# Queries directly behind the outputs, all eight tiles of values together behind the scores

## What is computed

```
xn = group_norm(x, gamma, beta)            # 32 groups, eps 0.001
q = xn @ wq + bq;  k = xn @ wk + bk;  v = xn @ wv + bv
scores = einsum('bnc,bmc->bnm', q, k) * C ** (-0.5)
attn = softmax(scores, axis=-1)
out = einsum('bnm,bmc->bnc', attn, v)
out = out @ wp + bp + x
```

## Time and profile before

| | |
|---|---|
| median of three runs | 2090.53 us (2090.38 to 2091.23) |
| the profiled execution, its own time | 2090.45 us |
| its span, first to last instruction | 2088.7 us |
| PE busy | 2082.3 us, 9214 matmuls |
| DVE busy | 1734.4 us |
| ACT busy | 746.2 us |
| POOL busy | 535.0 us |

### The profile page before, as it was taken

The page is one execution under the profiler, slowest core; times in us unless marked ns, Lnnn a source line. Parts: engine busy times, 40 slices in busy tenths (PEclk is TensorE's granted clock), DMA queues, the critical chain, the costliest instruction groups (busy, mean ns, idle before and its releaser), DMA issues.

```text
span 2088.7 us, 28028 instructions
## 1 busy us (share of the span) xinstructions
PE 2082.3 (100%) x9214; PEld 1724.0 (83%) x9214; DVE 1734.4 (83%) x2838; ACT 746.2 (36%) x1225; POOL 535.0 (26%) x236
## 2 busy tenths in 40 slices
PE   9999999999999999999999999999999999999999
PEld 7888888888888888888888888888888888888887
DVE  7997888878889788897878888788887888878864
ACT  5332423335233252333423333243333523325231
POOL 1323123322132212322223231322322213221230
PEclk9999999999999999999999999999999999999999
DMA  7212030120301203021120211203012030120201
GB/s 177 61 51 71 6 91 25 50 70 10 109 2 57 63 15 105 0 80 40 34 87 0 80 40 50 70 0 92 28 50 70 10 98 13 50 70 14 67 1 61
DMA packets 110331, 108.13 MB, mean 52 GB/s; under 512 B 8540, under 2 KB 74080, under 8 KB 110304
## 3 DMA queue, kind: packets, MB, share of 16 engines
q1 hardware_dynamic: 108544, 104.63, 16.8%
q10 hardware_dynamic: 1760, 3.15, 0.6%
HBM read 74.19 MB, written 33.55 MB: 52 GB/s over the span
## 4 chain that ended last, share of the span: by engine, by line
PE 99%; DVE 1%; DMA 0%; issue 0%; SPq 0%; ACT 0%; DVEq 0%
PE psum L1375 11%; PE psum L1376 11%; PE psum L1377 11%; PE psum L1356 11%; PE psum L1358 11%; PE psum L1357 11%; PE psum L1141 6%; PE psum L1143 6%; PE psum L1142 6%; PE psum L1245 5%; PE psum L1244 5%; PE psum L1242 5%; DMA w_k<-in_L_conv_wk_dram 0%; PE psum L1196 0%; PE psum L1198 0%; PE psum L1197 0%
## 5 line engine op out<-in xcount | busy, mean ns | idle before, releaser
L449 POOL TENSOR_TENSOR x_res<-x_res,out_bias 128x512 f32<-128x512 f32 x124 | 216.1, 1766 | 895.9 <-PE psum L1245 451.0
L1375 PE MATMUL psum<-v_hi,pt_hi 128*128 128x512 f32 x1024 | 398.4, 389 | 0.0
L1376 PE MATMUL psum<-v_lo,pt_hi 128*128 128x512 f32 x1024 | 398.3, 389 | 0.0
L1377 PE MATMUL psum<-v_hi,pt_lo 128*128 128x512 f32 x1024 | 398.3, 389 | 0.0
L585 ACT ACTIVATE score<-psum 128x512 f32<-128x512 f32 x256 | 152.8, 597 | 325.1 <-PE psum L1358 325.0
L1375 PEld LDWEIGHTS psum<-v_hi,pt_hi 128*128 128x128 f32 x1024 | 192.2, 188 | 39.9
L1377 PEld LDWEIGHTS psum<-v_hi,pt_lo 128*128 128x128 f32 x1024 | 192.2, 188 | 39.9
L1376 PEld LDWEIGHTS psum<-v_lo,pt_hi 128*128 128x128 f32 x1024 | 192.2, 188 | 39.9
L1356 PE MATMUL psum<-pt_hi,xn_hi 128*128 128x512 f32 x512 | 199.5, 390 | 0.4 <-DVE v_lo L834 0.4
L1358 PE MATMUL psum<-pt_hi,xn_lo 128*128 128x512 f32 x512 | 199.2, 389 | 0.0
L1357 PE MATMUL psum<-pt_hi,xn_hi 128*128 128x512 f32 x512 | 199.2, 389 | 0.0
(11 more groups left out here) (184 smaller groups left out, 3942.6 us busy)
## 6 DMA issues: line engine op xcount, KB each, us to landing
x_res<-in_x_dram SPq DMA_DIRECT2D x128, 256.0 KB, 2.9
out_dram<-x_res SPq DMA_DIRECT2D x128, 256.0 KB, 2.1
x_blk<-in_x_dram SPq DMA_DIRECT2D x240, 128.0 KB, 2.8
score<-in_x_dram SPq DMA_DIRECT2D x16, 128.0 KB, 6.7
w_q<-in_L_conv_wq_dram ACTq DMA_DIRECT2D x6, 256.0 KB, 10.8
w_v<-in_L_conv_wv_dram SPq DMA_DIRECT2D x1, 1024.0 KB, 5.8
w_p<-in_L_conv_wp_dram SPq DMA_DIRECT2D x1, 1024.0 KB, 9.3
w_k<-in_L_conv_wk_dram ACTq DMA_DIRECT2D x4, 256.0 KB, 9.0
```

What stands on the lines that cost most here:

```text
L449: last = nc.gpsimd.tensor_tensor(at, at, out_bias[:, first:end], ALU.add)
L1375: nc.tensor.matmul(dst, hi[:, m, queries], v_hi[:, m, :], start=m == 0, stop=False)
L1376: nc.tensor.matmul(dst, hi[:, m, queries], v_lo[:, m, :], start=False, stop=False)
L1377: end = nc.tensor.matmul(dst, lo[:, m, queries], v_hi[:, m, :], start=False, stop=m == NT - 1)
```

## The change

Only the order is changed, and what follows from it for banks and semaphores; no instruction is added or dropped but waits.

- In every image the values of tiles 0 and 1 are moved from in front of the queries to the front of the other six, behind the scores, on PE, ACT and DVE.
- In image 0 the two halves of the queries so stand directly behind one another. Both now use `work[0]` to `work[3]`, and chunk j of the second half waits for `first_query_lo(0, j)`.
- The banks of the later queries are renamed so that each still precedes the score tile that uses the same bank. Waits on `v_lo` in the queries fall away but for the first; a wait for the whole `xn_lo` takes the place of the one that tile 0 of the values had.
- On DVE in image 0, `m_lo` parts 2 and 3 are made behind all first queries and `xn_lo`; and the four `first_query_lo(1, j)` stand ahead of the four `row_part(0, j)` and are no longer interleaved with them.

```
-        USES = ([("v", 0, m) for m in range(2)] + [("s", h, m) for h in range(NH) for m in range(NT)]
-                + [("v", 0, m) for m in range(2, NT)])
+        USES = [("s", h, m) for h in range(NH) for m in range(NT)] + [("v", 0, m) for m in range(NT)]
...
         def first_bank(h, j):
-            return work[(2 * h + j) % 4]
+            return work[j]
...
             def first_queries():
                 first_query_lo(0, 0)
-                setup_lo_parts(SET_M, m_hi, m_lo, 3, KC)
                 first_query_lo(0, 1)
                 second_lo_parts()
                 first_query_lo(0, 2)
                 first_query_lo(0, 3)
-                v_lo_part(0, 0)
-                v_lo_part(0, 1)
+
+                setup_lo_parts(SET_M, m_hi, m_lo, 2, KC)
                 block_sums_of_a()
...
                 for j in range(KC):
                     first_query_lo(1, j)
+                for j in range(KC):
                     row_part(0, j)
...
                     else:
 
                         pe.wait_ge(s_free, n * SPLIT)
+                        pe.wait_ge(s_xl, (n + 1) * KC)
                     block_product(BANK_1, A11, p, xn_hi, xn_lo, 0, 0)
...
                 for j in range(KC):
-                    if j < 2:
-                        pe.wait_ge(s_tl, j + 3)
-                    else:
-
-                        pe.wait_ge(s_free, j - 1)
+
+                    pe.wait_ge(s_tl, j + 1)
...
                 if starts(b):
                     first_half_queries()
-                v_tile(b, 0)
-                v_tile(b, 1)
-                if starts(b):
                     second_half_queries()
                 else:
                     queries(b)
                 for m in range(NT):
                     score_tile(b, 0, m)
                 for m in range(NT):
                     score_tile(b, 1, m)
-                for m in range(2, NT):
+                for m in range(NT):
                     v_tile(b, m)
```

More of the change, by code:

```diff
@@ L246, in group_norm_attention @@
         assert NU % 4 == 0 and NU == SPLIT + SCORES
-        BANK_1, BANK_6, BANK_7, BANK_5 = work[2], work[3], work[0], work[1]
+        BANK_1, BANK_6, BANK_7, BANK_5 = work
         def final_half(n, h):
@@ L661, in image @@
                     bias_products()
-                v_hi_part(b, 0)
-                v_hi_part(b, 1)
-                if starts(b):
                     for j in range(KC):
@@ L1020, in _ @@
             sum_products(0, KC)
-            setup_lo_parts(SET_M, m_hi, m_lo, 2, 3)
             def block_sum(at, left, right, op):
@@ L1059, in image @@
                 else:
-                    v_lo_part(b, 0)
-                    v_lo_part(b, 1)
                     queries(b)
@@ L1088, in image @@
                         pt_lo_parts(b, 0, 2 * m - 6, 2 * m - 4)
-                for m in range(2, NT - 1):
+                for m in range(NT - 1):
                     if starts(b):
@@ L1216, in work_bank @@
                         pe.wait_ge(signal, value)
-                elif what in (("v", 0, 0), ("v", 0, 1)) and starts(n):
-                    pe.wait_ge(s_tl, 1 + what[2])
                 elif not (before and starts(n)):
@@ L1229, in v_tile @@
                 ready = ()
-                if m == 0:
-                    ready = ((s_setr, lo_rank(SET_M)),) if starts(n) else ((s_xl, n * KC),)
+                if m == 0 and starts(n):
+                    ready = ((s_setr, lo_rank(SET_M)),)
                 product(dst, [(xn_hi[:, k, chunk(m)], xn_lo[:, k, chunk(m)], m_hi[:, k, :], m_lo[:, k, :])
@@ L1272, in queries @@
                     else:
-                        pe.wait_ge(s_free, n * SPLIT + 1)
                         pe.wait_ge(s_xsl, earlier(n) * 4 + 2)
@@ L1278, in queries @@
                     else:
-                        pe.wait_ge(s_free, n * SPLIT + 2)
                         pe.wait_ge(s_xsl, earlier(n) * 4 + 3)
@@ L1370, in out_tile @@
                         pe.wait_ge(s_ptl, (n * NH + h) * NT + m + 1)
-                    if i == 0 and m > 1:
+                    if i == 0:
                         pe.wait_ge(s_free, n * SPLIT + PLACE[("v", 0, m)] + 1)
```

## The result

| | before | after |
|---|---|---|
| median of the runs | 2090.40 us (8 runs, 2090.01 to 2091.23) | 2097.22 us (8 runs, 2096.04 to 2099.09) |
| the profiled execution | 2090.45 us | 2097.24 us |
| its span | 2088.7 us | 2095.5 us |
| mean granted clock of PE over the span | 1.000 | 0.998 |

The changed kernel is slower: the ratio is 1.0033, with a 95% interval of 1.0024 to 1.0043. The forecast was 2096.2 us, in a range of 2093.4 to 2098.3. So direction and size were right, and 1.0 us is missing in the sum.

A forecast was written before the change was run, and what follows sets the result against it. PE, busy without a gap, was taken to bound the kernel. Against 2090.45 us: 4.67 wait + 0.11 restart + 0.16 for `xn_lo` - 0.68 old waits = 4.3, plus 1.5 clock, 5.8: 2096.2 us, range 2093.4 to 2098.3.

The forecast's parts named there:

- What bounds the kernel: From 66 to 1980 us PE is busy without a gap, so every new wait of PE is added in full.
- The wait at the first scores: Image 0: PE wants the first scores at 57.03, DVE's lo part releases them at 61.70; 4.67 us, plus 0.11 restart.
- `xn_lo`: Image 0, start of the second half's queries at 45.99: PE waits for `xn_lo` part 1, 0.16 us lost, bounds 0 and 0.4.
- The bound of 3.5: Image 0, first scores: the wait is 3.5 us if POOL blocks DVE's sums but not its products.
- rival 1: Image 0: the wait comes, but the clock doesn't fall (2094.7) or products aren't blocked (2093.6; both, up to 2094.9); chance 0.20.
- The clock: Image 0: PE's clock falls in the wait; some 3 us at half speed lose 1.5 us, bounds 0 and 2.6.
- The old waits of 0.68: Image 0, around the first scores: PE's present waits, together 0.68 us, go.
- The loop: Images 1 to 15: no new wait of PE, 0 us; smallest slack 1.4 us, `u2` 1.1 us late within DVE's idle 1.39.
- Rivals 3 and 4: Loop: DVE's race with POOL turns around in 14 images, 2099.0, chance 0.07; the 5.44 us cover was needed, 2103.7, 0.05.
- rival 4: Loop: the 5.44 us cover was needed, `xs_lo` or `u2` over 1.4 us late; 0.5 per image, 2103.7; chance 0.05.
- I count nothing: Image 0 after the first-scores wait: DVE 1.4 us earlier, its lag grows by no more than 0.3 us; no loss counted.
- rival 2: Image 0: DVE finishes its four sums before POOL holds the ports; wait 0.3, 2090.2 with `xn_lo` in time; chance 0.05.

The follow-up runs named there:

- the third experiment: The changed kernel with GpSimd's four additions of the output bias held back until VectorE's five products are done; 2092.16 us, ratio 1.0008.
- the first experiment: The changed kernel with the second half's first two lo parts put ahead of the five products on DVE; 2092.47 us, ratio 1.0009.
- `e9_copy_first`: The changed kernel, image 0: two second-half lo parts before the products, `xn_lo` before the first half's second lo part, ACT's copies before exponentials; 2091.27 us.
- the second experiment: The changed kernel with 36 transposes without use on PE between the second half's queries and image 0's first scores; 2094.72 us, ratio 1.0022.

## Why the prediction was right, and where it was off

- **What bounds the kernel**: right. PE had nothing to give back; the last matmul is 6.8 us later, and so is the end.
- **The wait at the first scores**: due at 57.03, measured 57.27, since PE lost 0.32 for `xn_lo` where the forecast had 0.16 (DVE began it at 45.41 and not at 45.29), and 0.08 more in small spacings behind it. Released at 61.52 where 61.70 was forecast. 4.26 for 4.67. Four blocked instructions were counted, and there were four; but the steps said that DVE would win one sum and lose three and one product. It won three sums in a row and lost one and three products. The step that failed is that POOL's first addition would come in between two sums of DVE, as L490 had done in before. The totals agree because in both orders DVE waits once for each of POOL's four additions; that the order of the steps didn't matter was luck.
- **That products are blocked too** was taken from the kind of their inputs alone, with 3.5 us as the bound if they were not. The rows show it three times (1.78, 1.68 and 1.63 for 0.69). The bound of 3.5, and that part of rival 1, fall.
- **The clock**: right that it falls, mis-sized. 1.5 was forecast, 2.73 and (in the experiment) 2.50 to 2.72 were measured, just beyond the bound of 2.6. I had taken about the lowest of 2.8 to 5.2 us from the program's start; PE ran 5.9 us at the lower level behind the wait. Against the forecast's sum of 5.8 this term is 1.2 too low, `xn_lo` 0.16 too low and the wait 0.4 too high: the missing 1.0.
- **The old waits of 0.68 go**: right.
- **The loop**: right. The first scores of images 1 and 15 of the changed kernel stand at 192.26 and 1982.01, that is 14 x 127.84, and from 68 to 1980 PE has no gap. DVE's idle time behind `u2` fell from 1.39 to 0.40, where the forecast left 0.3. Rivals 3 and 4 didn't come; rival 4's border, "a DVE 1.4 us behind its place", was too far: by the experiments it lies at 0.6 to 0.8, counted from the end of `xs_lo`, and PE then waits for `u` (L854) and not for `xs_lo`.
- **Image 0 behind the wait**: "I count nothing" held in the changed kernel, but only because the first wait was there. The tile whose slack was 2.4 us in before had 3.9 in after (99.78 behind 95.87), since PE, pushed back by 7, came there 1.4 later than in before. Of DVE's "1.4 us earlier" 0.2 were left at the shifted scores (93.42 for 93.60). The slack of that tile was not among the rows I read, and the price of rival 2, the case without the wait, is wrong for it. Had rival 2 come true, the time would have been 2092.2, as the third experiment shows, and not 2090.2. The experiments make the faster side weaker still than the 0.02 that it had.

## What to carry to other kernels

Work that is moved away from between two dependent stages was cover for every engine that feeds the second stage, and not for the one alone that you look at: read the slack of each later tile of the same image (when its releaser ended, when it started) before you say what mending the first wait would give. Where two engines' lists contend, count the blocked instructions as a total and don't trust their order; and look at what the engine that you moved away meets later. A wait of an engine that is otherwise never idle costs more than its length if the clock falls in it: here 4.3 us cost 7.1.

## What the runs showed of the chip

- A back-to-back row of DVE instructions with two inputs in SBUF can keep POOL waiting through several of them: POOL's L486, started 0.02 us behind the first of three in after and 0.24 behind it in the first experiment, took 3.02 and 2.80 us in place of 1.29. It is no rule. L490 of before (1.73 us) and L487 of `e9_copy_first` (1.74 us), each directly behind another POOL instruction, waited for one sum and came in ahead of the next. In the trace of the second experiment POOL's L486 even stands 0.01 us ahead of the sum (50.30 and 50.31) and takes 3.06, so at such distances the rows don't tell who is first. In the other direction DVE's sum waits for one POOL instruction and then has its turn. The Trainium skill's "SBUF — State Buffer" (two separate sides) lets whichever starts first have the ports for the whole instruction; the rows of DVE's waits agree, and POOL's rows show that "the other" does not always come next when DVE has its following instruction ready.
- DVE's custom product instruction, which reads two inputs in SBUF, is blocked by POOL like a tensor_tensor (1.63 to 1.78 us for 0.69). `first_query_lo`, with an input in PSUM, was not: in the first experiment two of them ran from 53.77 to 55.17, beside POOL's L487 (53.26 to 55.01), and took 1.40 us together, as two of them do elsewhere (1.41 at 60.90).
- The granted clock fell some 3.1 us behind the end of PE's last matmul before the wait (60.6 against 57.43) and stood at 0.5, the level of 1.2 GHz, for 6.8 us; a 128x512 matmul started every 0.427 us there, and every 0.227 at full clock. Transposes of 128x128 in the wait kept it at 1.00.
